# Reordered prologue of an adapter and conditional linear kernel: ids first, table turned later, other order on GpSimd, three of four first norms on ScalarE

## The reference

```python
# for each sample, with l = itok_B_0_8[s], g = itok_B_0_30[s]
h = relu(x @ W1[l] + b1[l])                      # 512 -> 128
y = x + (h @ W2[l] + b2[l])                      # 128 -> 512
normed = (y - mean(y)) * rsqrt(var(y) + 1e-5)    # over the features
x = x + (normed * gamma[l] + beta[l])
x = x + (x @ W[g] + b[g])                        # 512 -> 512
```

## Time and profile before

| | |
|---|---|
| median of 3 runs | 640.29 us (639.36 to 640.73) |
| the profiled execution, its own time | 639.83 us |
| its span | 638.0 us |
| TensorE (PE) busy | 628.6 us, 99% |
| VectorE, GpSimd, ScalarE busy | 529.3, 413.7, 404.1 us |
| last wait of TensorE on another engine's work | at 46.1 us |
| halves of x of k0, issue to landing | 4.7 us (SyncE), 5.3 us (ScalarE, issued at 0.71 us) |

### The profile page before, as it was taken

One profiled execution on the slowest core, in us unless ns is written; L12 is line 12 of the kernel. 1 busy time (PEld: TensorE's weight loads), 2 busy tenths in 40 slices (PEclk: granted clock), 3 DMA queues, 4 the chain that ended last, 5 costly groups with the idle time before them and its releaser, 6 DMA issues.

```text
span 638.0 us, 11207 instructions
## 1 busy us (share of the span) xinstructions
PE 628.6 (99%) x2797; PEld 487.1 (76%) x2797; DVE 529.3 (83%) x1157; ACT 404.1 (63%) x707; POOL 413.7 (65%) x326
## 2 busy tenths in 40 slices
PE   9799999999999999999999999999999999999997
PEld 7568777778777778777778777777877777877786
DVE  1879888889888889888889888889888889888873
ACT  3657566767565767666767665767666666666670
POOL 2877667666676676677676676676676676667630
PEclk9999999999999999999999999999999999999999
DMA  7948899888898888899798898988899887899422
GB/s 214 324 118 263 275 309 275 252 255 288 273 320 259 260 258 277 284 305 282 255 247 283 280 301 266 273 261 268 285 292 294 254 257 272 278 290 314 164 83 99
DMA packets 125562, 166.00 MB, mean 260 GB/s; under 512 B 10834, under 2 KB 72284, under 8 KB 121456
## 3 DMA queue, kind: packets, MB, share of 16 engines
q1 hardware_dynamic: 93540, 149.59, 72.0%
q10 hardware_dynamic: 32012, 16.30, 10.5%
HBM read 132.17 MB, written 33.55 MB: 260 GB/s over the span
## 4 chain that ended last, share of the span: by engine, by line
PE 92%; DVE 2%; POOL 1%; DMA 1%; issue 1%; ACT 1%; SPq 0%; ACTq 0%; DVEq 0%; POOLq 0%
PE o_bank L707 18%; PE o_bank L705 18%; PE o_bank L706 18%; PE d_bank L732 16%; PE n_bank L721 9%; PE d_bank L707 2%; PE d_bank L705 2%; PE y_bank L705 2%; PE y_bank L707 2%; PE d_bank L706 2%; PE y_bank L706 2%; DMA w_raw<-in_L_cond_W 1%; DMA ids<-in_itok_B 1%; POOL x_tok L350 1%; DVE y L562 0%
## 5 line engine op out<-in xcount | busy, mean ns | idle before, releaser
L368 POOL TENSOR_TENSOR w_lo<-w_raw,w_hi 128x512 fp32r<-128x512 f32 x128 | 162.2, 1289 | 106.3 <-ACT w_hi L416 106.3
L705 PE MATMUL o_bank<-w_hi,x1T_hi 128*128 128x512 f32 x512 | 205.2, 401 | 0.0
L707 PE MATMUL o_bank<-w_hi,x1T_lo 128*128 128x512 f32 x512 | 200.4, 391 | 0.0
L706 PE MATMUL o_bank<-w_lo,x1T_hi 128*128 128x512 f32 x512 | 199.6, 390 | 0.0
L350 POOL TENSOR_TENSOR x_tok<-x_tok,b_bc 128x512 f32<-128x512 f32 x128 | 163.2, 1298 | 45.3 <-DMA b_bc<-in_L_cond_b 43.3
L607 DVE SCALAR_TENSOR_TENSOR n_bank<-n_bank,params,xT 128x512 f32<-128x512 f32 x128 | 93.3, 753 | 61.5 <-PE n_bank L721 61.5
L442 ACT ACTIVATE squares<-y,neg_mean 128x512 f32<-128x512 f32 x128 | 91.7, 717 | 76.1 <-DVE neg_mean L568 76.1
L550 DVE STREAM_TRANSPOSE xT<-x_quad 128x512 f32<-128x512 f32 x120 | 127.3, 1106 | 3.1 <-issue 3.1
L732 PE MATMUL d_bank<-xT,w_raw 128*128 128x512 f32 x256 | 115.9, 594 | 1.6 <-DVE xT L550 1.6
L707 PEld LDWEIGHTS o_bank<-w_hi,x1T_lo 128*128 128x128 f32 x512 | 96.1, 188 | 20.7
L705 PEld LDWEIGHTS o_bank<-w_hi,x1T_hi 128*128 128x128 f32 x512 | 97.0, 189 | 18.0
(11 more groups left out here) (60 smaller groups left out, 568.5 us busy)
## 6 DMA issues: line engine op xcount, KB each, us to landing
w_raw<-in_L_cond_W SPq DMA_DIRECT2D x32, 1024.0 KB, 6.5
out<-out_half SPq DMA_DIRECT2D x63, 512.0 KB, 3.4
x_tok<-in_x SPq DMA_DIRECT2D x31, 1024.0 KB, 8.8
w_raw<-in_L_cond_W SPq DMA_DIRECT2D x64, 256.0 KB, 7.1
b_bc<-in_L_cond_b SPq DMA_DIRECT2D x64, 256.0 KB, 9.3
x_quad<-in_x SPq DMA_DIRECT2D x60, 256.0 KB, 3.9
x_quad<-in_x ACTq DMA_DIRECT2D x60, 256.0 KB, 3.9
x_tok<-in_x ACTq DMA_DIRECT2D x1, 512.0 KB, 5.3
```

Of the source, the lines that this page charges most:

```text
L368: pool.tensor_tensor(w_lo[q][:, c, :], w_raw[q][:, c, :], w_hi[q][:, c, :].bitcast(F32), ALU.subtract).then_inc(w_lo_done, 1)
L705: pe.matmul(acc, lhs_hi, rhs_hi, start=first, stop=False)
L706: pe.matmul(acc, lhs_hi, rhs_lo, start=False, stop=False)
L707: return pe.matmul(acc, lhs_lo, rhs_hi, start=False, stop=last)
```

## The change

SyncE loads the language ids ahead of the half of x; b1 goes behind W2; x of k1 goes ahead of the wait for the category ids and so ahead of W; b2 of k1 goes ahead of W2 of k1. TensorE issues 12 products of zeros instead of 16 at the start, goes from the transposes of x of k0 straight to up, turns the table behind it, then turns x of k1 (before: behind down of k0), and then does down of k0; the 8 products of zeros between up and down are gone. The high part of the first W2 is made by ScalarE instead of VectorE. GpSimd, in its first two steps, adds b2 to tiles 0 and 1 of k1 ahead of the identity addition and to tiles 2 and 3 ahead of the low parts of W. ScalarE makes three of the first four norms. The loop's own order is as it was, but for two waits of GpSimd that have changed places.

```diff
--- before.py
+++ after.py
@@ -281,23 +281,23 @@
                     store(k, 2, 1)
 
 
+            sp.dma_start(ids[0:1, 0, :], lang_ids.rearrange("(o s) -> o s", o=1)).then_inc(lang_in, 16)
             sp.dma_start(x_tok[0][:, 0:2, :], x_rows[0, :, 0:2, :]).then_inc(first_x_in, 16)
-            sp.dma_start(ids[0:1, 0, :], lang_ids.rearrange("(o s) -> o s", o=1)).then_inc(lang_in, 16)
             sp.dma_start(ids[0:1, 1, :], cat_ids.rearrange("(o s) -> o s", o=1)).then_inc(cat_in, 16)
             sp.wait_ge(lang_in, 16)
             lang0 = sample_id(0, 0, L)
             load_w1(lang0, 0)
+            load_b2(lang0, 0)
+            load_w2(lang0, 0)
             sp.dma_start(params[0][:, 2 * NC:NP], b1[bass.ds(lang0, 1)].rearrange("o a -> a o")
                          ).then_inc(first_b1_in, 16)
-            load_b2(lang0, 0)
-            load_w2(lang0, 0)
+            load_x(1, 1)
             sp.wait_ge(cat_in, 16)
             load_w(sample_id(1, 0, G), 0)
             lang1 = sample_id(0, 1, L)
-            load_x(1, 1)
             load_w1(lang1, 1)
+            load_b2(lang1, 1)
             load_w2(lang1, 1)
-            load_b2(lang1, 1)
             sp.wait_ge(table_done, 1)
             sp.dma_start(params[0][:, 0:2 * NC],
                          param_table[:, bass.ds(lang0, 1), 0:2 * NC].rearrange("p o n -> p (o n)")
@@ -337,8 +337,7 @@
             def step(h, p, adapter=True, turn=True, follow=True):
 
                 k, q = Step(h, p), 1 - p
-                if turn:
-
+                def plus_identity():
                     pool.wait_ge(w_in[q], 16 * k.pairs(1) + 16)
                     raw = w_raw[q][:, :, :]
                     blocks = bass.AP(raw.tensor, raw.offset, [[NC * H, P], [H + 1, NC], [NC, P]])
@@ -347,29 +346,46 @@
                                        ALU.add).then_inc(diag_done, 1)
 
                 def plus_b2(t):
+                    if t == 0:
+                        pool.wait_ge(x_in[p], 16 * k.pairs(0) + 16)
+                        pool.wait_ge(b2_in[p], 16 * k.pairs(0) + 16)
+                        if not k.since(2):
+                            pool.wait_ge(first_xT_turned, k.count(NC, 0, NC))
                     pool.tensor_tensor(x_tok[p][:, t, :], x_tok[p][:, t, :], b2_bc[p][:, :],
                                        ALU.add).then_inc(x_b2_done, 1)
 
-                if adapter:
-
-                    pool.wait_ge(x_in[p], 16 * k.pairs(0) + 16)
-                    if not k.since(2):
-                        pool.wait_ge(first_xT_turned, k.count(NC, 0, NC))
-                    pool.wait_ge(b2_in[p], 16 * k.pairs(0) + 16)
+                def low_w(c):
+                    if c % 2 == 0:
+                        pool.wait_ge(w_hi_done, k.count(2, 1, c // 2 + 1))
+                    pool.tensor_tensor(w_lo[q][:, c, :], w_raw[q][:, c, :],
+                                       w_hi[q][:, c, :].bitcast(F32), ALU.subtract).then_inc(w_lo_done, 1)
+
+                if not k.since(2):
+
                     plus_b2(0)
                     plus_b2(1)
-                if turn:
-
-                    for c in range(NC):
-                        if c % 2 == 0:
-                            pool.wait_ge(w_hi_done, k.count(2, 1, c // 2 + 1))
-                        if c == 2 and not k.since(2):
-                            low_w2(1, 2)
-                        pool.tensor_tensor(w_lo[q][:, c, :], w_raw[q][:, c, :],
-                                           w_hi[q][:, c, :].bitcast(F32), ALU.subtract).then_inc(w_lo_done, 1)
-                if adapter:
+                    if turn:
+                        plus_identity()
                     plus_b2(2)
                     plus_b2(3)
+                    if turn:
+                        low_w(0)
+                        low_w(1)
+                        low_w2(1, 2)
+                        low_w(2)
+                        low_w(3)
+                else:
+                    if turn:
+                        plus_identity()
+                    if adapter:
+                        plus_b2(0)
+                        plus_b2(1)
+                    if turn:
+                        for c in range(NC):
+                            low_w(c)
+                    if adapter:
+                        plus_b2(2)
+                        plus_b2(3)
                 if follow:
                     low_w2(q, k.count(1, -1, 1))
 
@@ -496,6 +512,7 @@
             for c in range(NC):
                 act.wait_ge(first_xT_turned, c + 1)
                 act.activation(xT[0][:, c, :], first_xT_bank(c)[:, :], ACT.Copy).then_inc(xT_done, 1)
+            high_w2(0, 0)
             relu(k0)
             for t in range(NT):
                 square(k0, t)
@@ -505,6 +522,7 @@
 
             normalise(k1, 0)
             normalise(k1, 1)
+            normalise(k1, 2)
             load_next_x_quads(k1)
             relu(k1)
             high_w(k1, 2)
@@ -656,8 +674,6 @@
 
 
             k0, k1 = Step(0, 0), Step(0, 1)
-            dve.wait_ge(w2_in[0], 16)
-            dve.tensor_copy(w2_hi[0][:, :], w2_raw[0][:, :]).then_inc(w2_hi_done, 1)
             dve.wait_ge(w2_hi_done, 1)
             dve.tensor_tensor(w2_lo[0][:, :], w2_raw[0][:, :], w2_hi[0][:, :].bitcast(F32), ALU.subtract
                               ).then_inc(w2_lo_done, 1)
@@ -672,7 +688,7 @@
             inverse_deviation(k0)
 
             dve.wait_ge(rstd_done, 1)
-            for t in (2, 3):
+            for t in (3,):
                 dve.tensor_scalar(norm[:, t, :], y[:, t, :], rstd[:, t:t + 1], neg_mean_rstd[:, t:t + 1],
                                   ALU.mult, ALU.add).then_inc(norm_done, 1)
             x1(k1, 0)
@@ -783,10 +799,11 @@
                 ins.then_inc(first_xT_turned, 1)
 
             pe.wait_ge(zeros_done, 1)
-            keep_clock(16, y_bank[1])
+            keep_clock(12, y_bank[1])
             pe.wait_ge(ident_done, 3)
             for c in range(NC):
                 turn_first_x(k0, c)
+            up(k0)
             pe.wait_ge(rows_in, 48)
             for n in range(NP):
                 first, step_of = (n // NC * H + n % NC, NC) if n < 2 * NC else (2 * H, 1)
@@ -794,12 +811,10 @@
                                    param_rows[:, first:first + (P - 1) * step_of + 1:step_of],
                                    ident[0:L, 0:L])
             ins.then_inc(table_turned, 1)
-            up(k0)
-            keep_clock(8, y_bank[1])
+            for c in range(NC):
+                turn_first_x(k1, c)
             pe.wait_ge(table_done, 1)
             down(k0)
-            for c in range(NC):
-                turn_first_x(k1, c)
             up(k1)
             keep_clock(4, o_bank[1])
             turn_norm(k1, 0)
```

## The result

| | median | executions |
|---|---|---|
| before | 640.73 us | 7, 637.91 to 641.21 |
| changed | 636.08 us | 7, 635.77 to 637.50 |

The ratio is 0.9940 (95% interval 0.9922 to 0.9958): faster by 0.6%, 3.8 us by the ratio and 4.6 by the medians, where 0.5 us was forecast.

The account below looks back on a forecast made before the run. TensorE bounds the loop, so only the prologue counts, through the start of down of k1: 29.5 instead of 30.02, -0.5 us, loop and tail 0. From the median 640.29 that gives 639.8 us, range 638.1 to 641.9.

Parts of the forecast that it names:

- What bounds: TensorE fills the loop; the end moves one for one with VectorE's prologue transposes, 12.3 us after down of k1 starts.
- the hole: Empty and low DMA windows behind x of k0, from the wait for the ids; removing them gains 1.9 us.
- All later loads come 1.8 us sooner: Prologue loads shift by 1.8 us; with reordering, x of k1 lands at 14.4 and b2 of k1 at 18.6.
- order, forecast: Going ahead of W brings x of k1 2.5 us sooner; going ahead of W2 brings b2 of k1 0.6 sooner.
- Down of k0: On TensorE in the prologue, starts at 16.5 against 16.58, behind the transposes of x of k1.
- All that was won in front is spent on waiting for x of k1: TensorE, ready at 13.0, waits until 14.4 and transposes for 2.1 us, so down of k0 barely moves.
- GpSimd's new wait: Identity addition waits for b2 of k1 until 22.7, delaying ScalarE; gives back a third of the third norm's gain, leaving 0.5.
- Norms, table, fillers: Prologue: ScalarE's three norms take 2.2 us; the table behind up gives 1.1; 24 filler rows end near 6.1.
- the two gaps ahead of down of k1 stay as long: TensorE's idling of 1.24 and 1.70 us remains, so down of k1 keeps its lowered clock and 4.44 us.
- Rival (a): Down of k1 starts at 29.0 and runs at full clock: 2.6 us won, 637.7; clock alone 638.2; chance 0.23.
- (b): Ids still wait behind ScalarE's half of x, down of k1 starts at 31.3: +1.3 us, 641.6; chance 0.10.
- (c): TensorE slow in front, from a late clock rise or a fall behind the wait for x of k1: +2, 642.3; chance 0.17.

Follow-up runs that it names:

- loads alone: Kernel before with only the changed kernel's SyncE load order: 639.38 us, ratio 0.9994; with 8 products of zeros ahead of down of k1 as well, 637.73 us.
- ids second: Changed kernel with SyncE's half of x loaded ahead of the language ids again: 639.08 us, ratio 0.9989.
- down of k0 first: Changed kernel plus 8 products of zeros ahead of down of k1, with down of k0 ahead of the transposes of x of k1: 641.06 us, ratio 1.0023.
- filled changed kernel: Changed kernel plus 8 products of zeros in TensorE's gap ahead of down of k1: 635.71 us, ratio 0.9941.
- b1 ahead: Changed kernel with b1 of k0 loaded ahead of b2 and W2 again: 636.61 us.
- e15b: Filled changed kernel with SyncE's loads in the order of before: 643.71 us, ratio 1.0075.
- e11: Filled changed kernel with GpSimd's order of before and down of k0 ahead of the transposes of x of k1: median 636.33 us.
- e9: Apparently the filled changed kernel with down of k0 ahead of x of k1's transposes and GpSimd's identity addition ahead of its k1 additions: 636.72 us.

## Why the prediction was wrong

*What bounds.* Right. The end followed VectorE's transposes one for one (4.03 and 4.1 us), and these followed down of k1; the loop stayed as it was. The experiments confirm it: in each of the 15 traces in which that down ran wholly at full clock, the execution's time less the start of down of k1 is 608.2 to 608.3 us, whatever had been moved in front. With the lowered clock it is 609.8 (the kernel before) and 610.7 (loads alone).

*The loads: the step that failed.* The forecast cut out the hole and shifted the rest as a block: "All later loads come 1.8 us sooner", x of k1 at 14.4, b2 of k1 at 18.6. They landed at 11.7 and 15.6. Both terms of that sum were too small, as ids second, which has the hole and the new order, tells:

| | before | ids second | changed | order, forecast | order, measured | hole, forecast | hole, measured |
|---|---|---|---|---|---|---|---|
| x of k1 lands | 18.7 | 14.6 | 11.7 | 2.5 | 4.1 | 1.8 | 2.9 |
| b2 of k1 lands | 21.0 | 18.4 | 15.6 | 0.6 | 2.6 | 1.8 | 2.8 |

These are single traces. In the other traces that have the ids first x of k1 lands from 11.4 to 12.7 and b2 of k1 from 15.3 to 16.4, so the hole is worth 1.9 to 3.2 us; in the four with the loads of before they land from 18.7 to 19.1 and from 21.0 to 23.3, so the order is worth at least the 4.1 and 2.6, and its term is the surer miss. In the kernel before the windows from 8.5 to 12 us hold 94 to 246 GB/s, and I took them for the cost of these loads. Without a hole the windows from 5.5 to 12 us hold 259 to 463 GB/s. With the hole and the new order (ids second) the slow stretch is shorter, 168 to 246 GB/s from 9 to 11 us. So a part of it belongs to the order. b1 is the suspect: in the four traces that have a hole and b1 ahead of b2, b2 of k0 took 4.5 to 5.1 us from issue to landing, in ids second, which has b1 behind W2, 3.7. b1 ahead of b2 was tried alone only without the hole, where it changes nothing. Why transfers behind an empty queue are slow for some microseconds, and whether b1 adds to it there, stays open.

*Down of k0.* Forecast 16.5, bound by x of k1; measured 14.93, with no wait. "All that was won in front is spent on waiting for x of k1" is false by this one number.

*GpSimd's new wait.* Forecast to give back a third; it gave back nothing. The identity addition ended at 19.7 and ScalarE needed it at 20.6. That ScalarE waits when this addition is late is real, as down of k0 first shows (3.57 us of waiting), but here it has 0.9 us of cover, since b2 of k1 is sooner. Put the measured landings in the forecast's own chain and it comes out: statistics at 14.93 + 7.4 = 22.3, norms 2.2, to down 2.93, so 27.5 against 27.55.

*Norms, table, fillers.* Taken singly out of the filled changed kernel they cost 0.7, 0.7 and 0.6 us, and GpSimd's order 0.2. That these come to 2.2, near the 2.0 to 2.2 between the kernels at full clock, must not be read as a sum: ids second, taken out singly, costs another 1.6, the loads alone bring 0.1, and without the loads the others lose 5.8 us. The loads lift the bound, the others use the room. That W2's high part is made by ScalarE now was never taken back alone, so what it is worth is not shown.

*The clock.* This is the second term that failed. The forecast left down of k1 at its 4.44 us, because "the two gaps ahead of down of k1 stay as long"; it took 2.88, though the gap of 1.70 us had stayed to the hundredth (the one ahead of it had shrunk from 1.24 to 0.41). Rival (a) named the clock and priced it right, 1.6 us, but even its whole sum, 637.7, lies above the 636.1, for it kept the late landings. Five of seven executions had no lowered clock. The forecast's error was to take one profiled execution for the kernel. 62 in 100 executions of the kernel before have a lowered clock, at +1.5 or +2.7 us; the medians' difference of 4.6 is 2.0 of order and the rest of clock (in the profiled pair 2.47 and 1.56). How much of that rest belongs to the change is not settled, for b1 ahead, nearly the same kernel, had 5 of 10 below full clock, though none at 0.995.

*The rivals.* (b) failed: SyncE waited 0.6 us for the ids. (c) did not occur, but e15b and ids second are what it described, a clock lowered in front behind a wait for x of k1: in both traces, and by the clock of the whole span in all five and in seven of ten executions. The clock fell during or behind idling of 5.10 us (e15b), 3.83 us (down of k0 first), 1.70 us (loads alone) and 1.03 us (e11), and did not fall at gaps of 1.72 and 1.70 us in the changed kernel's trace, nor at the gap of 1.03 us ahead of down of k0 in that of e9. The Trainium skill ("TensorE: Matmul & The Clock Gate", Part 1) says that the clock falls again when the array idles: the falls agree, and the gaps without one show that a gap of the same length does not always bring it. It says too that the clock rises only with sustained activity: the fillers' step from 421 to 275 ns each agrees, the granted clock of 1.00 in the same windows does not show it.

## What to carry to other kernels

A hole in the transfers ahead of a dependent load can cost more than its length (here 2.8 for 1.9 us), so put the small load that everything hangs on first in its queue, and don't forecast its removal as a mere shift. Cost a reordered prologue as a maximum of chains and recompute every landing first; single steps are worth little until the bound above them is lifted, and can be worth less than nothing. When executions of one kernel fall into groups by the granted clock, compare within the groups, and fill the gap ahead of the product that suffers: eight products of zeros took 1.4 us off the kernel before by the medians, 2.0 by the ratio. Fill it before the clock can fall; behind a long wait the same filler cost time.

## What the runs showed of the hardware that was not expected

- Behind a hole of 1.9 us and with b1 ahead of b2 the loads of the kernel before moved at 94 to 246 GB/s for 3.5 us, with the DMA share up to 1.54; behind the same hole with b1 behind W2 (ids second) at 168 to 246 GB/s for 2 us; without the hole no window of the changed kernel between 2.5 and 15 us fell below 259 GB/s.
- The products of zeros at the start go from 421 to 275 ns each at a moment that differs from trace to trace: 32 rows of them took from 5.19 to 6.60 us. The granted clock in the windows there is 1.00 throughout.
- 62 of 100 executions of the kernel before had a lowered clock over the span. In the two traces that show it, it fell at the gap of 1.70 us ahead of down of k1, inside it (loads alone) or 0.6 us behind it (the kernel before), and with the gap filled none of 10 executions had it; the changed kernel has a gap of the same length and no fall in its trace. When the clock fell inside the gap it stayed low through all of down (5.29 us instead of 2.88).
